# Layer norms spread over three slots, the projection over two, and the importance split given its own buffer

## The reference

```python
def _L0_conv_ref(x, ...):                       # x is already normalised per image and channel
    y = conv(x, conv_w, padding=15, rhs_dilation=5)            # 7x7, 32 channels to 1
    imp = sigmoid(gelu(batch_norm(y)))                         # importance of each pixel
    xs = x * imp
    idx = sort(top_k(imp[:, 0].reshape(B, -1), 192))           # 192 tokens per image
    tokens = take_along_axis(xs, idx) + make_pos(H * H, C)[idx]
    q, k_, v = split(tokens @ w_qkv.T + b_qkv, 3)              # 8 heads of 4
    o = (softmax(q @ k_.T / sqrt(4)) @ v) @ w_o.T + b_o
    t1 = _layernorm(tokens + o, ln1_g, ln1_b)
    ff = relu(t1 @ w1.T + b1) @ w2.T + b2
    t2 = _layernorm(t1 + ff, ln2_g, ln2_b)
    return xs with the rows idx replaced by t2
x = x + _L0_conv_ref(_gn(x), ...)                # _gn: (x - mean) / sqrt(var + eps) per channel
```

## Time and profile before

| what | value |
|---|---|
| three runs | 1154.83, 1157.81, 1164.65 us; median 1157.81 us |
| the profiled execution | 1156.72 us, of which the span of the profile is 1154.8 us |
| PE busy | 944.7 us, 82% of the span |
| DVE busy | 841.7 us, 73% |
| ACT busy | 769.4 us, 67% |
| POOL busy | 636.3 us, 55% |
| granted TensorE clock | mean 0.901 of 2.4 GHz |

### The profile page before, as it was taken

One profiled execution on the slowest core, in us unless ns is written; L12 is line 12 of the kernel. 1 busy time (PEld: TensorE's weight loads), 2 busy tenths in 40 slices (PEclk: granted clock), 3 DMA queues, 4 the chain that ended last, 5 costly groups with the idle time before them and its releaser, 6 DMA issues.

```text
span 1154.8 us, 21628 instructions
## 1 busy us (share of the span) xinstructions
PE 944.7 (82%) x6440; PEld 743.1 (64%) x6440; DVE 841.7 (73%) x2114; ACT 769.4 (67%) x1899; POOL 636.3 (55%) x853
## 2 busy tenths in 40 slices
PE   3887977599968997999899989898787688389676
PEld 2665655377747875787687868785665477277544
DVE  5345779478858986898789988896697589466654
ACT  2445654287747895888678877886588487178443
POOL 5332234832676468647774687458545764772542
PEclk9898989799989998999899999999899599689755
DMA  9998978575655999899898989876565466448778
GB/s 244 280 293 235 279 210 236 144 190 157 167 149 157 264 260 247 230 261 279 239 263 249 262 265 264 249 211 161 152 182 146 121 175 184 121 118 237 204 237 264
DMA packets 176677, 247.90 MB, mean 215 GB/s; under 512 B 65937, under 2 KB 72433, under 8 KB 176561
## 3 DMA queue, kind: packets, MB, share of 16 engines
q1 hardware_dynamic: 168368, 244.11, 75.3%
q0 software_dynamic: 8192, 2.40, 1.4%
HBM read 124.59 MB, written 121.83 MB: 213 GB/s over the span
## 4 chain that ended last, share of the span: by engine, by line
PE 41%; DVE 19%; POOL 10%; ACT 10%; DMA 9%; issue 9%; SPq 1%; ACTq 0%; POOLq 0%; DVEq 0%
PE cv L524 12%; PE sc L643 7%; PE xb L508 5%; PE pp L656 4%; PE tr L558 4%; DMA table<-xt 3%; POOL tok_imp L1006 3%; POOL tok_x L1006 3%; PE ib L571 3%; DVE res L1347 2%; POOL tok_pos L1006 2%; PE ms L672 2%; DMA X<-in_x 2%; ACT wgt L840 2%; ACT pr L869 2%
## 5 line engine op out<-in xcount | busy, mean ns | idle before, releaser
L524 PE MATMUL cv<-X,w_conv 128*128 128x330 f32 (+1 forms) x1024 | 302.4, 422 | 27.7 <-POOL X L980 25.7
L524 PEld LDWEIGHTS cv<-X,w_conv 128*128 128x128 f32 x1024 | 191.1, 201 | 63.7 <-issue 26.1
L840 ACT ACTIVATE wgt<-ib,eps_col,mom 128x440 f32<-128x440 f32 (+1 forms) x256 | 178.0, 702 | 41.0 <-DVE res L1347 27.5
L1142 DVE TENSOR_SCALAR_CACHE_REDUCE junk<-flat,th 128x385 bf16<-128x385 f32 x200 | 122.2, 611 | 105.6 <-ACT th L826 104.6
L508 PE MATMUL xb<-cst,X 128*110 128x128 f32 x900 | 151.0, 294 | 39.6 <-ACT xt L806 23.6
L1043 POOL TENSOR_SCALAR res<-res,mom 128x440 f32<-128x440 f32 (+1 forms) x152 | 96.4, 638 | 150.8 <-DVE res L1347 149.3
L643 PE MATMUL sc<-k_b,qm 128*128 128x192 f32 x768 | 166.2, 343 | 14.4 <-DVE pixf L1242 7.4
L806 ACT COPY xt<-xb 110x512 f32<-110x512 f32 x225 | 131.7, 585 | 47.8 <-PE xb L508 34.9
L869 ACT ACTIVATE pr<-sc,least 128x192 f32<-128x192 f32 x384 | 137.3, 416 | 16.0 <-DVE least L1311 14.9
L1347 DVE SCALAR_TENSOR_TENSOR res<-tr,mom,wgt 128x440 f32<-128x440 f32 (+1 forms) x192 | 122.0, 641 | 33.8 <-PE tr L558 26.0
L1123 DVE BATCH_NORM_STATS2 stats<-X 128x6 f32<-128x458 f32 (+3 forms) x256 | 139.5, 574 | 6.8 <-DMA X<-in_x 6.8
(11 more groups left out here) (172 smaller groups left out, 1533.5 us busy)
## 6 DMA issues: line engine op xcount, KB each, us to landing
table<-xt SPq DMA_DIRECT2D x240, 224.0 KB
rt<-table SPq DMA_DIRECT2D x240, 224.0 KB, 3.9
out<-res SPq DMA_DIRECT2D x320, 137.5 KB
X<-in_x SPq DMA_DIRECT2D x64, 412.5 KB, 5.1
X<-in_x SPq DMA_DIRECT2D x64, 343.8 KB, 5.6
conv_rows<-cvr SPq DMA_DIRECT2D x64, 188.0 KB
y<-conv_rows SPq DMA_DIRECT2D x64, 165.4 KB
out<-res SPq DMA_DIRECT2D x64, 68.8 KB
```

Of the source, the lines that this page charges most:

```text
L524: last = mm(cv[:, 0:CUT[half]], w_conv[:, 4 * q + z], X[:, m % XI, at0:at0 + CUT[half]], start=z == 0, stop=z == 3)
L840: last = A(wgt[:, n % 2, at0:at0 + w], ib[:, at0:at0 + w], ACT.Identity, scale=mom[:, NB * g + b, 2:3], bias=eps_col[:, 1:2])
L1142: v.tensor_scalar(junk[:, 0:FL], flat[:], th[:, 0:1], None, ALU.is_ge, ALU.add, accum_out=cnt[:]).then_inc(cnt_ok, 1)
```

## The change

It does five things.

1. `norm_first` is cut in three: `norm_in` (bias and residual), `norm_mean`, `norm_var`, in three slots that follow each other. NORM goes from 115 to 114 (slots 24, 25, 26), NORM2 stays at 120 (slots 0, 1, 2). POOL's `norm_last` goes from + 1 to + 3 (slots 27 and 3). New semaphores `y1_rd` and `y2_rd` are raised when `norm_in` has read `ms`; PE waits for these in place of `v1_ok` and `v2_ok`.
2. `project` is cut in two: q in slot 25, k and v in slot 26. For this EMBED goes from 82 to 81 (DVE's `embed` in slot 23, `tokens_turn` in slot 24), MIX from 114 to 113. SCORES stays at 87.
3. `im` is a buffer of its own. `find_rest` goes from slot 14 to 18, `split` from slots 23, 24, 25 to 28, 29, 0; the wait for the last split stands in `find_rest` now.
4. The mean is added by a table over the 30 slots of a round. It leaves the same 12 slots off POOL as before (2 to 5, 14 to 21), but in turns on ACT and DVE for all groups.
5. SCATTER and BACK with the loads around them come two slots later (scatters in slots 4 to 7; back from 9). The program has two slots more.

```diff
-        im = ce
+        im = sb("im", [H, NB, H])
...
-        qkv_ok = raised("qkv_ok")
+        qkv_ok = raised("qkv_ok", 2)
...
+        y1_rd = raised("y1_rd")
...
+        y2_rd = raised("y2_rd")
...
-        REST, SPLIT, PARTS_OUT = 74, (83, 84, 85), 87
-        EMBED, PROJECT, SCORES = 82, 86, 87
-        MIX, NORM, FEED, NORM2 = 114, 115, 118, 120
-        SCATTER, BACK, IMPB = 122, 127, (123, 127, 135, 142)
+        REST, SPLIT, PARTS_OUT = 78, (88, 89, 90), 92
+        EMBED, PROJECT, SCORES = 81, 85, 87
+        MIX, NORM, FEED, NORM2 = 113, 114, 118, 120
+        SCATTER, BACK, IMPB = 124, 129, (125, 129, 137, 144)
+
+        MEAN_ON = "PPADADPPPPPPPPDADADADAPPPPPPPP"
...
-        in_dmas = [(BACK + 1 + u - GATHER) % U < len(GATHERS) or (BACK + 1 + u - SCATTER) % U < 4 for u in range(U)]
-        adder = [[(DVE_ADDS if g >= G - 3 else ACT_ADDS) if in_dmas[u] else POOL_ADDS for u in range(U)] for g in range(G)]
+        adder = [[(POOL_ADDS, ACT_ADDS, DVE_ADDS)["PAD".index(MEAN_ON[(BACK + 1 + u) % U])] for u in range(U)] for g in range(G)]
...
-            def project(g):
-                pe.wait_ge(tokt_cp, upto(tokt_cp, g))
-                for p in range(2):
-                    for sem, value in sc_read[p][-1:]:
-                        pe.wait_ge(sem, value)
-                    sc_read[p].append((qk_cp, upto(qk_cp, g, p)))
+            def project(g, p):
+
+                if p == 0:
+                    pe.wait_ge(tokt_cp, upto(tokt_cp, g))
+                for sem, value in sc_read[p][-1:]:
+                    pe.wait_ge(sem, value)
+                sc_read[p].append((qk_cp, upto(qk_cp, g, p)))
+                last = mm(sc[:, p, 0:K], (wq, wk)[p][:], tok_t[:], start=True, stop=True)
+                if p == 0:
+                    last.then_inc(qkv_ok, 1)
+                    return
...
-                ms_read.append((v1_ok, upto(v1_ok, g)))
+                ms_read.append((y1_rd, upto(y1_rd, g)))
...
-            def norm_first(y, bias, res_in, out_v):
-
-                for half in range(2):
-                    post(v.tensor_tensor(out_v[:, halves[half]], y[:, halves[half]], rep[:, bias], ALU.add))
-                sync()
-                link(v.tensor_tensor(out_v[:], out_v[:], res_in[:], ALU.add))
+            def norm_in(g, y, bias, res_in, out_v, read):
+
+                post(v.tensor_tensor(out_v[:, halves[0]], y[:, halves[0]], rep[:, bias], ALU.add))
+                v.tensor_tensor(out_v[:, halves[1]], y[:, halves[1]], rep[:, bias], ALU.add).then_inc(read, 1)
+                dve.wait_ge(read, upto(read, g))
+                sync()
+                post(v.tensor_tensor(out_v[:], out_v[:], res_in[:], ALU.add))
+
+            def norm_mean(out_v):
+                sync()
...
+            def norm_var(out_v):
+                sync()
                 link(v.tensor_tensor(sq[:], out_v[:], out_v[:], ALU.mult))
...
-                for g, n in at(s, NORM + 1):
+                for g, n in at(s, NORM + 3):
                     pool.wait_ge(v1_ok, upto(v1_ok, g))
```

45 lines of the change are left out of this document (27 added, 18 removed).

## The result

The changed kernel takes 1152.0 us (median of 20 runs, 1147.0 to 1156.1); the kernel before, beside it, 1158.1 (20 runs, 1152.2 to 1164.7). The ratio is 0.994, 95% interval 0.993 to 0.996: about 6 us faster, a little under half of the 13.4 forecast, and inside the 1% that counts as no change. The profiled execution took 1153.4 us, span 1151.0.

What follows compares the result with a forecast made beforehand. With no engine over 92% busy, order and waits were taken to decide. Terms -6.0 (groups 2 to 5), +2, -5, -4.4, -2 and +2 sum to -13.4 us: 1144 against 1157.8, range 1133 to 1166 with the rivals.

Steps and rivals of the forecast that it cites:

- Slots 0 to 4: Second norm in thirds frees PE's sum, ACT's slot 3 add goes to DVE: 1.0 us in five rounds, -5 us.
- Groups 0 and 1: Both lose the cover of slot 24 without having waited long: +2 us for both, between 0 and 5.
- Groups 6 and 7: From the last landings: group 7 -3.8 us and -0.6 by its gathers; group 6 -2 after +0.6.
- The end: Two slots and three back units more, norms in the last group's way: +2 us, between -1 and +6.
- The embedding a slot earlier: Landing to slot 27's count, groups 2 to 5: 12.7 us becomes 11.5, -1.2 a round, between -2.6 and 0.
- Rival 1: Slower: slot 24 loses its cover and nothing is given back, 1.9 plus 0.6 in five rounds; 1172 us, chance 0.16.
- The clock: PE idles a slot earlier, less time at 1.2 GHz up to the back transposes: -0.9 us a round, between -1.9 and 0.
- The table: DVE adds four means in the gather slots: gathers +0.6 us for each of groups 0 to 6, -0.6 for group 7.
- The scatters stand two slots later: Scatters at slots 6 and 7 beside two means and a normalisation, POOL busy 78.64 of 120 us: costed at 0.
- Rival 3: No change: DVE's adds hold POOL's gathers and scatters, 1.8 us a round instead of 0.6; 1153 us, chance 0.12.
- Rival 2: No change: DMA queues full, gains in full rounds turn up as waits for `rt` or `xt`; 1158 us, chance 0.20.

Runs made afterwards that it cites:

- e_oldadd: The changed kernel with the old adders: means of the 12 slots on ACT for groups 0 to 4, on DVE for 5 to 7; 1141.2 us, ratio 0.986 to before.
- e_embed24: The changed kernel with embedding in slot 24, token turn in 25 and whole projection in 26, as before; 1148.2 us, ratio 0.989 to before.
- e_split: The kernel before with only the split's own buffer, the split in slots 28, 29, 0 and `find_rest` in 18; 1156.4 us, ratio 0.999.
- e_norm2: The changed kernel with the second norm in one slot, POOL's part a slot later, scatters and back units in old slots; 1145.9 us, ratio 0.992 to before.
- e_latescat: The changed kernel with the second norm in one slot, but scatters, read back and importance still two slots later; 1150.6 us, ratio 0.993 to before.
- e_hold: The changed kernel with one more POOL wait: image 1's second normalisation part waits for DVE's scans, from group 2 on; 1144.2 us, ratio 0.989 to before.
- t_taps: The changed kernel with SP's order alone changed: map read ahead of the `rt` read, one store behind it; 1142.4 us, ratio 0.986 to before.
- e_early: The changed kernel with the old adders in slots 2 to 5 alone; 1143.9 us, ratio 0.988 to before.
- after: The changed kernel itself, with nothing undone; 1152.0 us, ratio 0.994 to the kernel before.
- e_nosplit: The changed kernel with the split and `find_rest` in their old slots, the buffer still its own; 1171.8 us, ratio 1.013 to before.
- e_late: The changed kernel with the old adders in slots 14 to 21 alone; 1148.9 us, ratio 0.992 to before.
- e_holdb: The kernel before with POOL's normalisation made to wait for DVE's scans; 1161.8 us, ratio 1.002.
- e_besthold: The changed kernel with one-slot second norm, scatters, embedding and projection as before, old adders, and POOL's wait for the scans; 1143.6 us, ratio 0.987 to before.

## Why the prediction was half right

- **Slots 0 to 4, "-5": right.** 20.4 us became 19.2 in rounds 2 to 4, 1.2 a round against 1.0 forecast; 0.7 of it is ACT's add, as the old adders show.
- **Groups 0 and 1, "+2": wrong, it is -3.5.** Slots 82 to 90, of group 0, take 0.7 us less than before and slots 112 to 120, of group 1, 2.8 less.
- **Groups 6 and 7: right.** Group 7 has 8.7 us from its landing to its first scores against 12.0 (-3.3; "-3.8"), group 6 12.2 and 9.8 to its k copies (-2.4; "-2"). The changed kernel's timeline, which answers the earlier trace rows:

```profile
997.23 0.48 DVE L1293 TENSOR_TENSOR tok<-tok_x,pp 96x128 f32<-96x128 f32 x2 [13.52 <-DMA tok_pos<-in_pos,idx]
...
1005.95 0.92 PE L649 MATMUL sc<-k_b,qm 128*128 128x192 f32 x4 [0.68 <-ACT k_b L865]
```

- **The end, "+2": right.** 2.9 us by the profiles, from the last k copy on.
- **The embedding a slot earlier, "-1.2" a round: wrong, it is nothing.** Landing to k is 12.0 us after and 12.1 before. The terms were right one by one: the operations shrank (`tok<-tok,tok_pos` from 1.13 to 0.42, the norm's thirds stand apart), and slot 24's work lost its cover:

```profile
564.32 0.48 DVE L1293 TENSOR_TENSOR tok<-tok_x,pp 96x128 f32<-96x128 f32 x2 [4.53 <-DMA tok_pos<-in_pos,idx]
...
565.98 0.42 DVE L1300 TENSOR_TENSOR tok<-tok,tok_pos 96x256 f32<-96x256 f32 x1
...
568.98 0.61 DVE L1150 TENSOR_SCALAR_CACHE_REDUCE junk<-flat,th 128x385 bf16<-128x385 f32 x1
...
576.51 0.62 DVE L1150 TENSOR_SCALAR_CACHE_REDUCE junk<-flat,th 128x385 bf16<-128x385 f32 x1 [1.74 <-ACT th L832]
```

  From 564.32 to 576.51 are 12.2 us in this kernel's DVE timeline, still with a wait for ACT's refining at the end, as in the earlier trace rows. e_embed24, with the embedding back in slot 24, has the gains without the price and shows the size of each: -2.6 and +2.5. Rival 1 took 1.9 for the lost cover, and this is the 2.5. That its "1.9 plus 0.6" makes 2.5 too is luck: the 0.6 was the table's price at the gathers, which did not come. Its other half, nothing given back, was wrong.
- **The clock, "-0.9" a round: in part.** In the longer idle stretch before the landing PE is busy 2.28 of 5.50 us, as the window below shows; behind it, from 569 to 572, the granted clock is 0.50, the 1.2 GHz level, and from 572 on 0.99 (windows above). There is one dip where there were two, and it does not reach the back transposes of slot 27. Slots 27 to 0 take 11.5 us against 12.9 (rounds 2 to 4), 1.4 a round less; but e_split and e_norm2 have 11.6 too, and in round 4 the kernel before has 11.6, so what made two of the rounds of the kernel before dear there is not shown to be the clock.

```profile
560.50:566.00 5.50, 2.28 (x12) 1.48 (x12) 1.58 (x6) 1.65 (x4) 5.13 (x6) 1.00 0.41 117
```

- **The table, "+0.6" for the gathers: wrong in place and size.** The gathers did not change: POOL's 24 gathers of groups 6 and 7 in windows from the first to the last, now beside four DVE adds each (none and eight before):

```profile
875.80:905.40 29.60, 22.45 (x24) 0.96 0.47 125
966.10:996.00 29.90, 22.77 (x24) 0.87 0.48 123
```

  against 29.5 and 30.7 us in the earlier trace rows, so -0.8 in group 7 ("-0.6") and nothing in group 6. Yet the table costs 4 us alone and 10 in the changed kernel, most of it by DVE's two adds of slots 3 and 5. I had costed these by ACT's gain alone ("DVE has 1.9 us free, which takes the two thirds moved there"). That was true up to slot 4, and DVE is last from slot 4 on.
- **"The scatters stand two slots later ... and I cost that at 0": the step that failed.** Slots 4 to 8 measured +12.2 us in the profile. That is the cost of all that was moved there together, DVE's thirds and adds with it; the share of the scatters and BACK alone was not told from that of the norm's layout (e_norm2 and e_latescat). I had looked for POOL's lead and for PE's convolution waiting for it, and that did not come (28.2 us of waits against 25.7). What I had not followed are the two things that move with the scatters: BACK and its loads on SP's queue, with the map's read behind them, and POOL's normalisation, which did not come too late for PE but at the wrong time for DVE. The prediction also has the exclusion of DVE and POOL, but uses it only for the place in which the change removed such an overlap and for the gathers.
- **The rivals.** Rival 3 named the exclusion and priced it at the gathers, at 1153 us, which is nearly the time measured; but neither gathers nor scatters are longer. The place was the scans, and there POOL holds DVE, not DVE POOL. Rival 2 named DMA: what was gained did turn up as a wait for a transfer, but for one write and its read, with a DMA share of 0.73 and 0.69 in slots 4 to 8 of the changed kernel, not for want of bandwidth over the round.

**What is shown and what is argued.** Shown: in the changed kernel the meeting of scans and normalisation costs (e_hold, 6 to 7 us, by POOL's wait alone); SP's order costs (t_taps, 10 to 11 us), and in rounds 2 to 4, where the read ahead takes away the wait at `yy`, the stretch of the first four scans is gone with it; DVE's adds in slots 2 to 5 cost (e_early, 8 to 10 us). In the six kernels with the three-slot norm, without POOL's wait or the read ahead (after, e_nosplit, e_embed24, e_oldadd, e_early, e_late), 13 of the 18 rounds wait over 0.8 us at `yy` and 12 of these have stretched scans, while of the 5 with 0.7 us or less none has. Round 1 doesn't follow this: `yy` waits in none of the six, and the changed kernel and e_oldadd have stretched scans in it all the same, 4.2 us. Nor is the wait only the changed order's: e_holdb and e_besthold wait up to 2.0 us with the old one. That DVE, late by the wait, meets the normalisation just then is read from the timelines; the phase of the two was not set by itself. Why the map's write lands 9 us after its issue in round 4 with no store between stays open (the one-slot norm has 7.7 us without one, and no wait, as its read is issued earlier), and so does whether the adds in slots 14 to 21 cost anything.

## What to carry to other kernels

When a step moves, follow everything that is tied to it to the queue on which it is issued, and ask for each of the others on that queue who waits for it: where one read back stands among the stores and reads of its queue was worth more here than all the waits that this change removed. Whether two engines that exclude each other meet is a question of phase; a move that "costs nothing" may bring them together, and an idle wait on the engine with time to spare (POOL's 4.1 us) can be cheaper than the meeting. Where several repairs each give 6 to 11 us, look whether they act in the same slots before adding them up, and take sizes from medians, since one profiled execution may be a lucky one.

## What the runs showed of the hardware

- Four scans of 110 x 110 bf16, 1.46 us alone, take up to 4.8 us beside POOL's instructions on SBUF; DVE loses the whole of POOL's time (3.3 beside 3.2 us), POOL nothing. That is so where scatters stand just ahead of POOL's row; with the scatters in slots 2 to 5 no scan took over 1.30 us, and an instruction of the normalisation 1.45 in place of 1.25 (e_norm2).
- The read of the map, which SP issues when the write `conv_rows<-cvr` has landed, came 5.6, 7.8 and 9.7 us after the write in rounds 2, 3 and 4 of one kernel (e_oldadd), at the same place of its order.
- Executions of one kernel spread by up to 14 us (1137.5 to 1151.2 for e_embed24). The mean granted clock goes with it only in part: the changed kernel's lowest, 1147.0 us, and highest, 1156.1, ran at 0.912 and 0.908, but of 23 executions of the kernel before in one batch the fastest, 1150.5, ran at 0.911 and the slowest, 1163.7, at 0.899. One meeting of scans and normalisation more or less is 3 us by the scans' own rows; that it makes the spread is a guess.
